# The tails of three PNA layers: layer norm in two parts, row weights multiplied on another engine, bias in three matmuls

## The reference

```python
for l in range(3):
    # _pna_layer, cut: msg, four aggregates, three scalings, U, batch norm of u over the nodes
    u = (u - mu) / jnp.sqrt(v + BN_EPS) * bn_g + bn_b
    h = jax.nn.leaky_relu(u @ mix_w.T + mix_b, 0.01) + h
    mu = jnp.mean(h, axis=-1, keepdims=True)
    v = jnp.mean((h - mu) ** 2, axis=-1, keepdims=True)
    h = (h - mu) / jnp.sqrt(v + LN_EPS) * ln_g[l] + ln_b[l]
    h = jax.nn.elu(h)
```

## Time and profile before

| | us |
|---|---|
| median of 3 runs | 3643.06 |
| the runs | 3630.38, 3645.09, 3643.06 |
| the profiled execution | 3648.39 |
| its span | 3646.6 |
| PE busy | 2343.9 (64%) |
| DVE busy | 2200.4 (60%) |
| POOL busy | 1286.8 (35%) |
| ACT busy | 670.3 (18%) |

### The profile page before, as it was taken

One profiled execution on the slowest core, in us unless ns is written; L12 is line 12 of the kernel. 1 busy time (PEld: TensorE's weight loads), 2 busy tenths in 40 slices (PEclk: granted clock), 3 DMA queues, 4 the chain that ended last, 5 costly groups with the idle time before them and its releaser, 6 DMA issues. The chain is left out here.

```text
span 3646.6 us, 49155 instructions
## 1 busy us (share of the span) xinstructions
PE 2343.9 (64%) x11873; PEld 1324.4 (36%) x11873; DVE 2200.4 (60%) x6919; ACT 670.3 (18%) x1489; POOL 1286.8 (35%) x1342
## 2 busy tenths in 40 slices
PE   5999879997979965454447555454456654444563
PEld 2444345753636642222224322222234322222232
DVE  6998777473364565555556745455557555555566
ACT  0245621521031120000001400000003300000013
POOL 3000000002000046665652455555551556565640
PEclk8999989998979986777768876767778867676776
DMA  3123366264435554454441344444440544444521
GB/s 117 54 109 134 137 228 224 94 228 152 163 105 176 173 168 164 151 165 153 161 141 60 99 154 162 142 153 150 155 134 9 166 149 154 145 158 136 168 79 36
DMA packets 151740, 510.85 MB, mean 140 GB/s; under 512 B 32178, under 2 KB 51280, under 8 KB 150720
## 3 DMA queue, kind: packets, MB, share of 16 engines
q1 hardware_dynamic: 94254, 348.65, 27.2%
q0 software_dynamic: 43536, 93.43, 9.2%
q10 hardware_dynamic: 13826, 67.12, 4.6%
HBM read 278.95 MB, written 230.13 MB: 140 GB/s over the span
## 5 line engine op out<-in xcount | busy, mean ns | idle before, releaser
L677 POOL DMA_INDIRECT rows_g<-a_dram,idx_now x1173 | 1135.2, 968 | 1249.5 <-DMA a_dram<-g 494.8
L1754 PE MATMUL psum<-hs,slab 128*128 128x384 bf16 x6600 | 1197.5, 341 | 126.9 <-issue 78.1
L1754 PEld LDWEIGHTS psum<-hs,slab 128*128 128x128 bf16 x6600 | 672.6, 102 | 666.9 <-issue 285.7
L1200 DVE SCALAR_TENSOR_TENSOR run<-run,mask_pt,rows_g 128x128 f32<-128x128 f32 x1170 | 404.7, 346 | 289.7 <-issue 231.2
L1203 DVE SCALAR_TENSOR_TENSOR run<-run,mask_pt,rows_g 128x128 f32<-128x128 f32 x1170 | 402.9, 344 | 34.7 <-issue 23.7
L1691 PE MATMUL psum<-onehot_key,onehot_lane 128*128 128x512 bf16 (+1 forms) x1968 | 355.6, 338 | 23.3 <-issue 19.3
L1949 PE MATMUL psum<-w_U,vturned 128*128 128x384 f32 x150 | 116.0, 874 | 368.2 <-ACT vturned L1592 332.2
L1942 PE MATMUL psum<-identity,std_now 128*128 128x128 f32 x75 | 30.1, 401 | 495.3 <-ACT std_now L1584 454.0
L793 DVE TENSOR_SCALAR onehot_key<-key_row,key_at 128x1600 bf16<-128x1600 f16 x492 | 309.7, 630 | 0.0
L1584 ACT ACTIVATE std_now<-var_now,eps 128x128 f32<-128x128 f32 x75 | 30.1, 401 | 1326.4 <-DVE var_now L1162 864.9
L1691 PEld LDWEIGHTS psum<-onehot_key,onehot_lane 128*128 128x128 bf16 x1968 | 158.3, 99 | 204.4 <-issue 30.2
(11 more groups left out here) (329 smaller groups left out, 2898.3 us busy)
## 6 DMA issues: line engine op xcount, KB each, us to landing
slab<-at_part SPq DMA_DIRECT2D x200, 800.0 KB
scan_dram<-run SPq DMA_DIRECT2D x291, 512.0 KB
at_part<-part_now ACTq DMA_DIRECT2D x50, 800.0 KB, 4.0
sums_dram<-run ACTq DMA_DIRECT2D x43, 576.0 KB, 3.3
rows_g<-a_dram,idx_now POOLq DMA_INDIRECT x1173
rows_g<-in_attr SPq DMA_DIRECT2D x43, 148.5 KB
a_dram<-g SPq DMA_DIRECT2D x15, 320.0 KB, 2.9
agg<-sel_dram SPq DMA_DIRECT2D x3, 1600.0 KB
```

Of the source, the lines that this page charges most:

```text
L677: nc.gpsimd.indirect_dma_start(rows_g[:, slot, j, :], None, a_dram, bass.IndirectOffsetOnAxis(ap=idx_now[:, slot, j:j + 1], axis=0)).then_ ...
L1200: V.scalar_tensor_tensor(at[:, 0:D], before[:, 0:D], mark, rows, ALU.add, ALU.max).then_inc(s_run, 1)
L1754: T_.matmul(ps[:, 0:3 * D], counts[:, k * P:(k + 1) * P], hs[:, k, at:at + 3, :].rearrange("p s f -> p (s f)"), start=(k == 0), stop=False ...
```

## The change

In point 1 `row_three` goes, and the ones become 1/128; in point 2 each bank takes three bias matmuls, one for each part of the row, right behind its own products. In points 3 and 4 the first 15 blocks (`FORE`) are aggregated after bank 4's maximum and bank 3's statistics, get their square root, reciprocal and minus mean while banks 5 and 6 are still in work, and the last 10 follow. ScalarE normalises groups 0, 1 and 2; the square root of the last 10 blocks and the table of Exp come behind group 0. VectorE normalises groups 3 and 4 inside its loop over groups. GpSimd multiplies all five groups by the row of weights, and VectorE's loop starts from its result.

```diff
@@ gpsimd, behind the adds
+                gain = weights["L3_rows"][:, 3:4, :].to_broadcast([P, GB, D])
+                for i in range(NG):
+                    rows = agg[:, GB * i:GB * i + GB, :]
+                    if GB * i < FORE:
+                        pool.wait_ge(s_norm, FORE // GB * l + i + 1)
+                    else:
+                        pool.wait_ge(s_norm_late, (NG - FORE // GB) * l + i - FORE // GB + 1)
+                    nc.gpsimd.tensor_tensor(rows, rows, gain, ALU.mult).then_inc(s_gained, 1)
@@ vector
-                V.memset(ones16, 1.0).then_inc(s_ones16, 1)
+                V.memset(ones16, 1.0 / P).then_inc(s_ones16, 1)
...
-                step(V.tensor_tensor(row_lo, row_rest, row_mid, ALU.subtract))
-                step(V.tensor_scalar(row_three, row_hi, identity[:, 0:1], None, ALU.mult))
-                step(V.scalar_tensor_tensor(row_three, row_mid, identity[:, 1:2], row_three, ALU.mult, ALU.add))
-                V.scalar_tensor_tensor(row_three, row_lo, identity[:, 2:3], row_three, ALU.mult, ALU.add).then_inc(
-                    s_mix_row, 1)
+                V.tensor_tensor(row_lo, row_rest, row_mid, ALU.subtract).then_inc(s_mix_row, 1)
...
-                    if j:
+                    if j == 4:
+                        step(stats_of(j - 1))
+                        aggregate(0, FORE).then_inc(s_fore_mv, 1)
+                    elif j:
                         stats_of(j - 1)
+                    if j == 5:
+                        dve.wait_ge(s_fore_std, l + 1)
+                        step(V.reciprocal(rstd[:, 0:FORE], std[:, 0:FORE]))
+                        V.scalar_tensor_tensor(minus_mean[:, 0:FORE], mv[:, 0:FORE, 0], -1.0, rstd[:, 0:FORE],
+                                               ALU.mult, ALU.mult).then_inc(s_rstd, 1)
                 step(stats_of(NCB - 1))
...
+                aggregate(FORE, NB).then_inc(s_rows, 1)
@@ vector, loop over groups
-                        dve.wait_ge(s_norm, NG * l + i + 1)
-                        scaled = told_by(V.tensor_tensor(agg[:, now, :], agg[:, now, :], on_group(3), ALU.mult))
+                        dve.wait_ge(s_gained, NG * l + i + 1)
+                        shifted = told_by(V.tensor_tensor(agg[:, now, :], agg[:, now, :], on_group(4), ALU.add))
                     if 1 <= i <= NG:
                         ...
                     if i < NG:
-                        dve.wait_ge(s_dve, scaled)
-                        shifted = told_by(V.tensor_tensor(agg[:, now, :], agg[:, now, :], on_group(4), ALU.add))
-                    if i < NG:
                         dve.wait_ge(s_dve, shifted)
                         V.tensor_scalar(g[:, now, :], agg[:, now, :], 0.0, None, ALU.min).then_inc(s_y, 1)
+                    if i == 0:
+                        dve.wait_ge(s_std, S_LAYER * l + (S_X3 + 2))
+                        step(V.reciprocal(rstd[:, FORE:NB], std[:, FORE:NB]))
+                    if FORE + GB * i < NB:
+                        for b in range(FORE + GB * i, FORE + GB * i + GB):
+                            last = normalized(agg, agg)(b)
+                        last.then_inc(s_norm_late, 1)
@@ scalar
-                root_of(told(5), std[:], mv[:, :, 1], 0)
-                A.activation(cstd[:], ones[:, 0:1], ACT.Exp)
-                act.wait_ge(s_rstd, l + 1)
+                act.wait_ge(s_fore_mv, l + 1)
+                A.activation(std[:, 0:FORE], mv[:, 0:FORE, 1], ACT.Sqrt, bias=eps[:, 0:1]).then_inc(s_fore_std, 1)
...
+                act.wait_ge(s_rstd, l + 1)
                 normalize(0)
+                root_of(told(5), std[:, FORE:NB], mv[:, FORE:NB, 1], 0)
+                A.activation(cstd[:], ones[:, 0:1], ACT.Exp)
                 normalize(1)
...
-                    if i + 2 < NG:
-                        normalize(i + 2)
+                    if i == 0:
+                        normalize(2)
@@ tensor
-                    T_.matmul(..., ones16, row_three..., start=False, stop=True)
+                    for row in (row_hi, row_mid, row_lo):
+                        mm = T_.matmul(..., ones16, row..., start=False, stop=(row is row_lo))
...
-                    if j == 1:
+                    if j == 0:
                         pe.wait_ge(s_ones16, l + 1)
                         pe.wait_ge(s_mix_row, l + 1)
-                    if j:
-                        add_shift(j - 1)
-                add_shift(NCB - 1)
+                    add_shift(j)
```

More of the change, by code:

```diff
@@ L54 @@
 GB = 5
+FORE = 3 * GB
+TAKEN = 3
 NG = NB // GB
@@ L276, in gnn_kernel @@
         same = var_tmp[:].rearrange("p k f -> p (k f)")[:, 0:T]
-        row_hi, row_mid, row_lo, row_three = [var_tmp[:, 0:2, :].rearrange("p k f -> p (k f)")[:, i * D // 2:(i + 1) * D // 2]
-                                              .bitcast(BF16) for i in range(4)]
+        row_hi, row_mid, row_lo = [var_tmp[:, 0:2, :].rearrange("p k f -> p (k f)")[:, i * D // 2:(i + 1) * D // 2]
+                                              .bitcast(BF16) for i in range(3)]
         row_sum, row_rest = var_tmp[:, 2, :], var_tmp[:, 3, :]
@@ L369, in gnn_kernel @@
         s_rstd = sem("s_rstd")
+        s_fore_mv = sem("s_fore_mv")
+        s_fore_std = sem("s_fore_std")
+        s_norm_late = sem("s_norm_late")
+        s_gained = sem("s_gained")
         s_leaked = sem("s_leaked")
@@ L1291, in _, with aggregate @@
                 step(V.tensor_copy(row_mid, row_rest))
-                step(V.tensor_tensor(row_lo, row_rest, row_mid, ALU.subtract))
-                step(V.tensor_scalar(row_three, row_hi, identity[:, 0:1], None, ALU.mult))
-                step(V.scalar_tensor_tensor(row_three, row_mid, identity[:, 1:2], row_three, ALU.mult, ALU.add))
-                V.scalar_tensor_tensor(row_three, row_lo, identity[:, 2:3], row_three, ALU.mult, ALU.add).then_inc(
-                    s_mix_row, 1)
+                V.tensor_tensor(row_lo, row_rest, row_mid, ALU.subtract).then_inc(s_mix_row, 1)
+                def aggregate(lo, hi):
+                    for b in range(lo, hi):
+                        ins_ = V.bn_aggr(mv[:, b, :], stats[:, b, :])
+                    return ins_
                 def stats_of(j):
@@ L1308, in _ @@
                     V.tensor_tensor(rows, rows, ps, ALU.max).then_inc(s_leaked, 1)
-                    if j:
+                    if j == 4:
+                        step(stats_of(j - 1))
+                        aggregate(0, FORE).then_inc(s_fore_mv, 1)
+                    elif j:
                         stats_of(j - 1)
-                step(stats_of(NCB - 1))
[L1312 to L1317, removed]
+                    if j == 5:
[3 more added lines that the diff above has]
+                                               ALU.mult, ALU.mult).then_inc(s_rstd, 1)
+                step(stats_of(NCB - 1))
+                aggregate(FORE, NB).then_inc(s_rows, 1)
                 if l + 1 < LAYERS:
@@ L1333, in _ @@
                     if i < NG:
-                        dve.wait_ge(s_dve, scaled)
-                        shifted = told_by(V.tensor_tensor(agg[:, now, :], agg[:, now, :], on_group(4), ALU.add))
-                    if i < NG:
                         dve.wait_ge(s_dve, shifted)
                         V.tensor_scalar(g[:, now, :], agg[:, now, :], 0.0, None, ALU.min).then_inc(s_y, 1)
-                    if i >= 3 and l + 1 < LAYERS:
+                    if i == 0:
[5 more added lines that the diff above has]
+                        last.then_inc(s_norm_late, 1)
+                    if i >= TAKEN and l + 1 < LAYERS:
                         take_g(l + 1, i - 3)
@@ L2020, in add_shift @@
                     n = min(NB, 4 * j + 4) - 4 * j
-                    T_.matmul(bank(j)[:, 0:n * D].rearrange("p (b f) -> p b f", f=D), ones16,
-                             row_three.unsqueeze(1).to_broadcast([P, n, D]), start=False, stop=True,
-                             skip_group_check=True).then_inc(s_mixed, 1)
+                    for row in (row_hi, row_mid, row_lo):
+                        mm = T_.matmul(bank(j)[:, 0:n * D].rearrange("p (b f) -> p b f", f=D), ones16,
+                                      row.unsqueeze(1).to_broadcast([P, n, D]), start=False, stop=(row is row_lo),
+                                      skip_group_check=True)
+                    mm.then_inc(s_mixed, 1)
                 for j in range(NCB):
```

## The result

The change makes the kernel slower: 3691.13 us (median of 4 runs, 3683.51 to 3706.2) against 3644.07 (4 runs, 3630.38 to 3647.87) in the same comparison, ratio 1.0142 [1.012, 1.0163]. The forecast was 3656, range 3630 to 3668. The profiled execution of after took 3683.51 us around a span of 3681.7; the one of before spans 3646.6. So there are 35.1 us to find.

The account below looks back on a forecast made before the run. No engine was taken as full over the span; the tails' chains, largely VectorE-paced, count directly. Layers of +4.6, +4.6 and +4.2 sum to +13.4 us on the median 3643.06, giving 3656 us, range 3630 to 3668.

Parts of the forecast that it names:

- the change touches only the tails: Whole span: only the three layer tails, 122 us of 3646.6, would change in time.
- After the last `x` nothing changes: Behind each tail: copies, stores and gathers stay the same, so a shift of `x` passes on whole.
- Exclusion of GpSimd and VectorE: Group loops of the tails: GpSimd's multiplies and VectorE's two-input steps serialise, +13.4 us in sum; forecast case, chance 0.55.
- My walk: Layer 0's group loop, serialised: four multiplies of 1.53 on the path, last `x` at 2054.8, +4.6 us.
- Bias: Seven banks of a tail: first bank no earlier, second later, then 1.52 us a bank on PE; +0.85 us by bank 5.
- Norm in two parts: Tail's seam: group 0 normalised by 2031.2 instead of 2033.8, group 1 behind the table load, only 0.55 us earlier.
- The walk without exclusion: Group loops with both engines running freely: -1.1, -1.1 and -1.5 us by layer, -3.7 in sum.
- No exclusion: Rival at shift and elu beside GpSimd's multiply: no blocking, -3.7 us, 3639 us; chance 0.30.
- PE becomes the bound: Rival in the seven banks: low clock makes a bank 3.0 us against 1.55, +9 a layer, 3683 us; chance 0.07.
- The split gives all it can: Rival in the tails: group 1's lateness hidden, GpSimd's multiply 0.85, 6 us won a tail, 3625 us; chance 0.08.

Follow-up runs that it names:

- e4: The whole change but with the multiply by the row of weights back on VectorE, against the kernel before: 3637.35 us, ratio 0.9999.
- e9: The kernel before with only the norm in two parts, weights on VectorE and the old bias: 3680.15 us against 3687.03, ratio 0.9979.
- e2: The changed kernel with layer 1's VectorE loop moved five instructions later by fills: 3649.41 us, ratio 1.0046 to the kernel before.
- e7: The kernel before with layer 1's VectorE loop moved four instructions later: 3686.31 us, on a chip where before took 3685.87.
- e3: The kernel before with the bias edit alone, three bias matmuls a bank, norm and weights as before: 3642.97 us, ratio 1.0004.

## Why the prediction was wrong, point by point

**The step that failed** is the frame of the sum: "the change touches only the tails", and behind them "After the last `x` nothing changes". The order of work does not change there, but the place of the code does. The change makes layer 0's tail three VectorE instructions longer, and the loop behind it came to touch a fourth stretch of 128. I counted each instruction's microseconds and never asked where the instructions behind it come to lie. That is +40.8 us in the two profiles, against -5.7 for all the rest, which makes the 35.1 us of span. No rival had it either; every time that I gave lay in the tails.

What the trace of before could have told: its stretch of layer 1's loop has 9 instruction packets and is thus kept over its eleven turns, and a loop of 258 instructions is just longer than two stretches of 128. What it could not tell is where the borders lie; only a shifted kernel shows that. It was a risk with a chance, not something to forecast.

**Exclusion of GpSimd and VectorE: right in kind, priced too high.** This is the group loop of layer 0 in after, VectorE first:

```profile
2023.51 0.82 DVE L1346 TENSOR_TENSOR agg<-agg,w_L_rows 128x640 f32<-128x640 f32 x1 [1.46 <-POOL agg L715]
...
2025.03 2.60 DVE L957 TENSOR_SCALAR agg<-agg,mv,rstd 128x128 f32<-128x128 f32 x5
2027.54 0.81 DVE L1346 TENSOR_TENSOR agg<-agg,w_L_rows 128x640 f32<-128x640 f32 x1
2028.28 2.15 DVE L1349 SCALAR_TENSOR_TENSOR x<-g,agg 128x640 f32<-128x640 f32 x1
2030.35 1.83 DVE L1353 TENSOR_SCALAR g<-agg 128x640 f32<-128x640 f32 x1
2032.10 1.36 DVE L957 TENSOR_SCALAR agg<-agg,mv,rstd 128x128 f32<-128x128 f32 x5
2033.38 0.81 DVE L1346 TENSOR_TENSOR agg<-agg,w_L_rows 128x640 f32<-128x640 f32 x1
...
2036.13 2.02 DVE L1349 SCALAR_TENSOR_TENSOR x<-g,agg 128x640 f32<-128x640 f32 x1
```

and GpSimd's multiplies beside it:

```profile
2021.95 1.53 POOL L715 TENSOR_TENSOR agg<-agg,w_L_rows 128x640 f32<-128x640 f32 x1 [1.41 <-ACT agg L1647]
2025.64 1.64 POOL L715 TENSOR_TENSOR agg<-agg,w_L_rows 128x640 f32<-128x640 f32 x1 [2.16 <-ACT agg L1647]
2028.19 3.64 POOL L715 TENSOR_TENSOR agg<-agg,w_L_rows 128x640 f32<-128x640 f32 x2 [0.91 <-ACT agg L1647]
2033.54 3.94 POOL L715 TENSOR_TENSOR agg<-agg,w_L_rows 128x640 f32<-128x640 f32 x1 [1.71 <-DVE agg L957]
```

The multiply alone takes 1.53, as I took from the slope of the adds. Each of the four others goes with one stretched VectorE instruction: one of five normalisations (2.60 for the five instead of 1.36), an elu (2.15 instead of 0.81), a clamp (1.83 instead of 0.48), an elu (2.02), together 1.24 + 1.34 + 1.35 + 1.21 = 5.1 us. The last multiply in turn is held for 2.4 us (3.94 - 1.53) while shift, elu, clamp and shift run at their usual 0.81, 0.81, 0.48 and 0.81 in front of it. This is the forecast's picture, and it holds for instructions with one SBUF input too, which I had not asked. The section of the Trainium skill that the prediction drew on ("SBUF — State Buffer", "Who interferes with whom") names, beside the two-input instructions, one-input ones such as `tensor_scalar` in a mode with two ports; the stretched clamp agrees.

In e4, where the same loop has its multiplies on VectorE, nothing is stretched:

```profile
2023.07 0.82 DVE L1345 SCALAR_TENSOR_TENSOR x<-g,agg 128x640 f32<-128x640 f32 x1
2023.80 0.49 DVE L1349 TENSOR_SCALAR g<-agg 128x640 f32<-128x640 f32 x1
2024.20 1.37 DVE L949 TENSOR_SCALAR agg<-agg,mv,rstd 128x128 f32<-128x128 f32 x5
```

From the second aggregates' end to the last `x` after needs 21.03 us (2021.78 to 2042.81), e4 18.99 (2017.64 to 2036.63) and before 20.16 (2030.01 to 2050.17). So the split wins 1.2 and the multiply on GpSimd costs 2.0 on top: the 5.1 us of stretching, and 1.46 of waiting in front of the first shift, are not paid by the five multiplies of 0.82 that left VectorE. This part of a tail, unlike the one before it, hardly scatters. In sum over the three tails it is 59.5 to 59.6 us in all eleven profiles with before's norm, 55.7 in e4 and in e9, and 62.4 and 62.5 in after and e2. So behind the aggregates the split wins 3.8 us a run, GpSimd's multiplies cost 6.7, and the change +2.9; the forecast had some +9.7 there (13.4 less 1.24 a layer). My walk had four whole multiplies of 1.53 on the path, 6.1, and from the first shift to the last `x` 21.6 us; it is 19.3 (2023.51 to 2042.81). A multiply is charged by its overlap with what it holds, 1.2 to 1.35, and the time for which it is itself held was on nobody's path. That accounts for 1.0 of the 2.3; the rest isn't traced to one step.

**Bias: the pace right, the first banks not, and the price within the scatter.** The forecast had PE at 1.52 a bank; ScalarE's banks in after are 1.54 apart:

```profile
2008.48 0.60 ACT L1639 ACTIVATE agg<-psum 128x512 f32<-128x512 f32 x1 [4.38 <-PE psum L2046]
2010.02 0.60 ACT L1639 ACTIVATE agg<-psum 128x512 f32<-128x512 f32 x1 [0.94 <-PE psum L2046]
```

The first bank stands 5.05 behind the tail's begin in layer 0 (5.66 before), and 1.25 behind the row's last step, where I had said no earlier than 1.9: the first bias matmul began 0.15 behind the row and not 0.43, and the clock rose while the three ran (1.06 together; 0.81 in the next banks). In layer 1 they take 1.44:

```profile
2834.37 1.44 PE L2046 MATMUL psum<-var_tmp,vturned 128*128 128x512 bf16 x3
2835.60 1.90 PE L2053 MATMUL psum<-mix_now,edge_sum 128*128 128x128 f32 x8
2837.30 0.84 PE L2046 MATMUL psum<-var_tmp,vturned 128*128 128x512 bf16 x3
```

Granted clock there, as the earlier trace rows:

```profile
2834.00:2836.00 2.00, 2.00 (x7) 1.14 (x7) 0.22 (x1) 0.16 (x1) 0.00 (x0) 0.50 0.00 0
2836.00:2838.00 2.00, 2.00 (x12) 1.67 (x11) 0.69 (x1) 0.44 (x1) 0.76 (x1) 0.66 0.00 0
```

The second bank's eight products, which had lain under the wait for the bias row, here run at the 1.2 GHz level and take 1.90 instead of 1.05: the second bank is 2.35 behind the first there, and 2.63 in layer 0 of e4. In layer 0 of after the last aggregates end 18.35 behind the tail's begin, 18.27 before; the forecast was +1.24. In layer 1 they end 19.55 behind it.

But one profile of before is a poor measure here, as this part scatters by itself with the moment at which the clock rises: in layer 0 of e7 the granted clock is still 0.50 when the first bias matmul runs (0.63 us), and the last aggregates end 19.2 behind the tail's begin; in its layer 2 the clock is up by then (0.38 us), and they end 18.2 behind. In ten profiles with before's bias and norm (30 tails) the last aggregates end 18.0 to 19.3 behind the tail's begin, 18.6 in the mean; in e3's three tails 18.5 to 19.9 (19.3); with the split they end at 18.9 in the mean with the new bias (after, e2, e4) and at 19.0 with the old one (e9). So a price of 0.7 a layer may stand behind e3, and none is seen beside the split. In the times it is not seen either.

**Norm in two parts: right.** The first normalised group starts before the second aggregates end (2021.78) and ends 0.1 behind them, and the table load stands behind it, in front of group 1:

```profile
2019.84 2.03 ACT L1647 ACTIVATE agg<-agg,minus_mean,rstd 128x128 f32<-128x128 f32 x5 [1.64 <-DVE minus_mean L1332]
2021.82 0.30 ACT L1459 ACTIVATE std<-mv,eps 128x10 f32<-128x10 f32 x1
2022.14 1.28 ACT L1654 ACT_TABLE_LOAD   x1
```

The walk without exclusion had given -1.1, -1.1 and -1.5 for a version in which GpSimd multiplies freely; e9, which multiplies on VectorE, shows 112.57 for three tails where those six profiles have 115.35 in the mean, so -2.8 (their scatter is 2.4), and -3.8 in the steady part behind the aggregates.

**The rivals.** "No exclusion" falls by the stretched rows. "PE becomes the bound" falls: at most the second bank is late, where the clock is low, and the others come 1.54 apart, not 3.0. "The split gives all it can" falls: group 1 did stand behind the table load, GpSimd's multiply took 1.53 and not 0.85, and no tail of after is shorter than before's. The tails' size, +4.7 in the profile of after and +5.2 in e2's, lies between the forecast's +13.4 and the rival's -3.7; +2.9 of it is steady, the rest is within the scatter of the first part.

**What stays open.** Which of the held stretches is given up when a fourth is needed, and why a turn then fetches five packets and not four or one. Five would fit if one stretch beyond the loop's four were always fetched ahead; no run tests that. The time of e2 is 0.46% above before, and its tails show a third to a half of that; the rest is within what two profiles of one kernel differ by.

## What to carry to other kernels

An edit also moves all code behind it on its engine. Where a long loop follows, count its instructions: VectorE's loop of 258 was kept at twenty places and not at two. By stretches of 128, of which a loop may touch three, one of up to 257 would always be kept and each instruction more would add one bad place in 128 (an estimate; lengths of 254, 256, 258 and 259 were run). The sign is in the profile: instruction packets that grow with the turns and an "issue" wait at the loop's head. When an edit makes a stretch slower that it does not touch, shift the kernel before by the same count before looking for any other reason. Beware of giving GpSimd work that lies beside a busy VectorE: four of the five multiplies here stretched an instruction by 1.2 to 1.35 us to spare VectorE 0.82. It depends on what lies beside it: the maxima, which read PSUM, take 0.69 each in after with and without one of GpSimd's adds beside them.

## What the runs showed of the hardware that I had not expected

- VectorE's loop of 258 instructions took 40.8 us longer over eleven turns when it began at 2370 (on the first chip 739 to 744 us at good places, 784 and 785 at this one). It was bad again at 2498 and at none of twenty other places of the loops of layers 1 and 2; one of 259 was bad at 2369, ones of 256 and 254 at 2370 were not.
- GpSimd's multiply was held for 2.4 us (3.94 instead of 1.53) while four VectorE instructions ran at their usual length; it got in at 2028.28, 2030.35 and 2036.13, each time stretching one VectorE instruction by 1.2 to 1.35. What decides this is open: at 2028.28 and 2030.35 VectorE had no pause either.
- The kernel before took 3639.08 us on one chip and 3685.87, 3687.03 and 3686.75 on three others. At good places and with the same 9 packets, layer 1's loop was 739 to 744 us long on the first and 752 to 760 on the others.
